# GNN layer 2: two of every 64 gathered tiles fetched by SP and ACT with one-row DMAs

## What is computed

```
h = maximum(layernorm(x), 0)
H = einsum('ni,rio->rno', h, W)
msg = (H[etype, src] + b[etype]) * weight
x = x + relu(segment_sum(msg, dst))
```

## Time and profile before

| | us |
|---|---|
| median of three runs | 8151.24 (8143.28 to 8152.59) |
| span of the profiled execution, first to last instruction | 8149.0 |
| PE busy | 6825.6 (84%) |
| POOL busy | 6074.5 (75%) |
| DVE busy | 3995.9 (49%) |
| ACT busy | 1919.9 (24%) |
| mean granted clock of TensorE | 0.932 |

### The profile page before, as it was taken

The page is one execution under the profiler, slowest core; times in us unless marked ns, Lnnn a source line. Parts: engine busy times, 40 slices in busy tenths (PEclk is TensorE's granted clock), DMA queues, the critical chain, the costliest instruction groups (busy, mean ns, idle before and its releaser), DMA issues.

```text
span 8149.0 us, 187072 instructions
## 1 busy us (share of the span) xinstructions
PE 6825.6 (84%) x52884; PEld 5276.0 (65%) x52884; DVE 3995.9 (49%) x13480; ACT 1919.9 (24%) x4919; POOL 6074.5 (75%) x6335
## 2 busy tenths in 40 slices
PE   5999999999999999999967777777778877777777
PEld 4666666666666666666646666666666666666665
DVE  7333333333333333333365555555555556555554
ACT  2333333333333333333330000000000000000001
POOL 5777777777777777777757777777777777777776
PEclk7999999999999999999979888888888888988898
DMA  6333333333333333333322222222222222222222
GB/s 141 82 83 82 81 83 82 83 82 83 82 83 82 82 83 82 83 83 82 82 61 53 53 53 53 53 53 52 53 53 53 53 52 53 52 53 53 53 53 72
DMA packets 797549, 566.94 MB, mean 70 GB/s; under 512 B 481443, under 2 KB 671019, under 8 KB 797292
## 3 DMA queue, kind: packets, MB, share of 16 engines
q0 software_dynamic: 200192, 256.65, 14.6%
q1 hardware_dynamic: 597340, 310.10, 14.5%
HBM read 544.45 MB, written 21.68 MB: 69 GB/s over the span
## 4 chain that ended last, share of the span: by engine, by line
PE 32%; issue 24%; POOL 21%; DMA 20%; DVE 1%; POOLq 1%; SPq 0%; ACT 0%; DVEq 0%; ACTq 0%
PE bank L1130 19%; POOL shared L549 17%; DMA shared<-p_tab,idx 11%; DMA rows_place<-h_tab,idx 6%; PE bank L1143 5%; POOL rows_place L549 4%; PE bank L1132 3%; DMA idx<-in_src_t 2%; PE bank L1054 2%; PE bank L1145 1%; PE bank L1061 1%; PE bank L1080 0%; DMA x_in<-in_x 0%; PE bank L1071 0%; DVE stats L744 0%
## 5 line engine op out<-in xcount | busy, mean ns | idle before, releaser
L549 POOL DMA_INDIRECT shared<-p_tab,idx x3128 | 2984.1, 954 | 959.8 <-issue 826.7
L549 POOL DMA_INDIRECT rows_place<-h_tab,idx x3128 | 2978.3, 952 | 964.3 <-issue 804.4
L1130 PE MATMUL bank<-shared,rows_place 128*128 128x256 f32 x6256 | 1842.2, 446 | 860.4 <-issue 748.1
L1130 PEld LDWEIGHTS bank<-shared,rows_place 128*128 128x128 f32 x6256 | 1296.4, 218 | 1126.6 <-issue 782.8
L959 DVE TENSOR_SCALAR shared<-iota_key,key,w_f 128x256 f32<-128x256 f32 x3128 | 1139.1, 425 | 745.3 <-PE bank L1132 633.1
L704 ACT ACTIVATE x_in<-bank 128x256 f32<-128x256 f32 x782 | 300.8, 385 | 3591.9 <-PE bank L1132 3264.7
L1061 PE MATMUL bank<-h_sb,w_tile 128*128 128x128 f32 x6256 | 907.7, 288 | 22.3 <-DVE h_sb L870 0.8
L1061 PEld LDWEIGHTS bank<-h_sb,w_tile 128*128 128x128 f32 x6256 | 758.5, 191 | 232.4 <-DVE h_sb L870 232.1
L1080 PE MATMUL bank<-wn_half,h_sb 128*128 128x128 f32 x6256 | 890.3, 285 | 0.0
L870 DVE TENSOR_SCALAR h_sb<-bank 128x128 f32<-128x128 f32 x782 | 228.2, 292 | 1315.8 <-PE bank L1054 1294.3
L1143 PE MATMUL bank<-x_in,w_rel_sb 128*128 128x64 f32 x6256 | 862.8, 296 | 0.0
(11 more groups left out here) (105 smaller groups left out, 5379.0 us busy)
## 6 DMA issues: line engine op xcount, KB each, us to landing
rows_place<-in_dst_c SPq DMA_DIRECT2D x782, 192.0 KB
shared<-in_edge_cols SPq DMA_DIRECT2D x782, 128.0 KB
shared<-p_tab,idx POOLq DMA_INDIRECT x3128
rows_place<-h_tab,idx POOLq DMA_INDIRECT x3128
idx<-in_src_t SPq DMA_DIRECT2D x1564, 2.0 KB
qr_w<-qr_tab SPq DMA_DIRECT2D x782, 18.0 KB
x_in<-in_x SPq DMA_DIRECT2D x14, 448.0 KB, 4.7
h_tab<-x_in SPq DMA_DIRECT2D x14, 448.0 KB, 3.0
```

Source lines behind the costliest of these rows:

```text
L549: pool.indirect_dma_start(out=rows_of[s][:, t, :], out_offset=None, in_=table, in_offset=bass.IndirectOffsetOnAxis(ap=idx[s][:, t:t + 1], ...
L1130: pe.matmul(bank[s][:, 0:RW], rows[s][:, t, :], hot_rel[s % 2][:, t, :], start=(t == 0), stop=(t == TC - 1))
```

## The change

In layer 2, the chunks are counted in groups of SUP = 16. In each group tiles 0 and 1 of chunk number 13 are no longer gathered by POOL. SP fetches tile 0 and ACT tile 1, row by row: for each chunk that either passes, it reads eight source numbers into registers with one call and issues eight DMAs, each of one row of h_tab to one partition. 16 such pieces fill a tile. The rows go to a place of their own with two halves, one for each of two successive groups (parts of h and hT, which layer 2 does not use). The source numbers come to partition 0 by a small strided DMA, issued by SP at chunk 5 of the group before. SP's last piece belongs to its step for chunk 13 (it waits for the slot's earlier scatter and issues the idx load first), ACT's to its step for chunk 12 (behind the copies of that chunk). Ahead of the loop SP issues two pieces and ACT three. 782 is 48 x 16 + 14, so the last chunk is such a chunk as well. The loops of SP, POOL, ACT and PE now hold 32 chunks in one turn; DVE's is unchanged.

```diff
+    SUP = 16
+    NSUP = NCH // SUP
+    ROWS = P // SUP
+    FED_AT, FED = 13, 2
...
+        fed_rows = h[0][:, 0:2 * FED, :].rearrange("p (k f) d -> p k f d", f=FED)
+        fed_ids = h[0][0:1, 2 * FED:3 * FED, :].rearrange("p f d -> p (f d)").bitcast(i32)
+        fed_ids = [fed_ids, hT[0:1, 0:FED * P].bitcast(i32)]
...
+        def feed(eng, f, lone, piece, landed):
+
+            _, at = nc.values_load_multi_w_load_instructions(
+                fed_ids[lone.half][0:1, f * P + piece * ROWS:f * P + (piece + 1) * ROWS], engines=(eng.engine,),
+                min_val=0, max_val=NPAD - 1, skip_runtime_bounds_check_because="a source node's number is below the number of nodes")
+            for k, row in enumerate(at):
+                p = piece * ROWS + k
+                eng.dma_start(fed_rows[p:p + 1, lone.half, f, :], h_tab[ds(row, 1), :]).then_inc(landed[lone.half], 16)
+
+        def feed_step(eng, f, lead, u, lone, after, landed):
+
+            first = FED_AT - lead - SUP + 1
+            if u - first < SUP:
+                feed(eng, f, lone, u - first, landed)
+            elif after:
+                if u == first + SUP:
+                    eng.wait_ge(fed_ids_landed, 16 * after.ids_turn + 16)
+                    hold(eng)
+                feed(eng, f, after, u - first - SUP, landed)
+
+        def feed_first(eng, f, lead, m, landed):
+
+            eng.wait_ge(fed_ids_landed, 16 * Lone(m, 0, 0).ids_turn + 16)
+            hold(eng)
+            for piece in range(SUP - 1 - FED_AT + lead):
+                feed(eng, f, Lone(m, 0, 0), piece, landed)
...
             def layer1_pass(m):
-                def step(c):
+                def load_ids(lone):
+                    sp.dma_start(fed_ids[lone.half], src_t[:, ds((lone.k * SUP + FED_AT) * TC, FED)].rearrange("p o -> o p"),
+                                 allow_slow_non_contiguous=True).then_inc(fed_ids_landed, 16)
+
+                def step(c, u, lone, after):
                     s = c.slot
                     sp.wait_ge(scattered[s], c.turn + 1)
                     hold(sp)
                     sp.dma_start(idx[s][:, :], src_t[:, ds(c.i * TC, TC)]).then_inc(idx1_landed[s], 16)
-
-                all_chunks(sp, m, step)
+                    if u == 5 and after:
+                        load_ids(after)
+                    feed_step(sp, 0, 0, u, lone, after, sp_row_landed)
+
+                load_ids(Lone(m, 0, 0))
+                feed_first(sp, 0, 0, m, sp_row_landed)
+                superchunks(sp, m, step)
...
+            def step1(c, u, lone, after):
+                gather(c, h_tab, rows, scattered, idx1_landed, rows_landed, range(FED if u == FED_AT else 0, TC))
+
             with pool.Fori(0, passes) as m:
-                all_chunks(pool, m, lambda c: gather(c, h_tab, rows, scattered, idx1_landed, rows_landed))
+                superchunks(pool, m, step1)
...
+                act.activation(w_sums[half][:, k, :], bank[c.slot][0:R, RW:RW + W], ACT.Copy)\
+                   .then_inc(sums_copied[c.slot], 1)
+                feed_step(act, 1, 1, u, lone, after, act_row_landed)
...
-                pe.wait_ge(rows_landed[s], 16 * TC * c.turn + 16 * TC)
+                pe.wait_ge(rows_landed[s], 16 * tiles_gathered(c, u, lone))
+                if u == FED_AT:
+                    pe.wait_ge(sp_row_landed[lone.half], 16 * P * lone.turn + 16 * P)
+                    pe.wait_ge(act_row_landed[lone.half], 16 * P * lone.turn + 16 * P)
```

More of the change, by code:

```diff
@@ L233, in gnn_two_layers @@
         pass1_ready, pass1_step = sem("pass1_ready"), sem("pass1_step")
+        fed_ids_landed, sp_row_landed, act_row_landed = sem("fed_ids_landed"), slot_sems("sp_row_landed", 2), slot_sems("act_row_landed", 2)
         block = ctx.enter_context(nc.Block())
@@ L270, in __init__ @@
                 self.m, self.slot, q = m, u % SL, quad + u // SL
+                self.quad = q
                 self.i = q * SL + self.slot
@@ L297, in paired, with __init__, superchunks @@
             step(None, at(NPAIR - 1), None)
+        assert NSUP % 2 == 0 and NCH == NSUP * SUP + FED_AT + 1
+        LONE_USES = [NSUP // 2 + 1, NSUP // 2]
+        class Lone:
+            def __init__(self, m, two, half):
+                self.m, self.half = m, half
+                self.k = two * 2 + half
+                self.turn = m * LONE_USES[half] + two
+                self.ids_turn = m * (NSUP + 1) + self.k
+        def superchunks(eng, m, step):
+            with eng.Fori(0, NSUP // 2) as two:
+                for half in range(2):
+                    for u in range(SUP):
+                        step(Chunk(m, two * (2 * SUP // SL) + (half * SUP + u) // SL, u % SL), u, Lone(m, two, half),
+                             Lone(m, two + half, 1 - half))
+            for u in range(NCH - NSUP * SUP):
+                step(Chunk(m, NSUP * SUP // SL + u // SL, u % SL), u, Lone(m, NSUP // 2, 0), None)
@@ new lines, in tiles_gathered @@
+        def tiles_gathered(c, u, lone):
+            if c.slot != FED_AT % SL:
+                return TC * c.turn + TC
+            return (c.m * (TC * SLOT_USES[c.slot] - FED * (NSUP + 1)) + lone.k * (TC * SUP // SL - FED)
+                    + (TC * (u // SL + 1) - FED * (u >= FED_AT)))
+        def feed(eng, f, lone, piece, landed):
[5 more added lines that the diff above has]
+                eng.dma_start(fed_rows[p:p + 1, lone.half, f, :], h_tab[ds(row, 1), :]).then_inc(landed[lone.half], 16)
@@ L540, in _, with gather @@
             pool.iota(pass_i[:, :], [[W, MAXPASS]], base=0, channel_multiplier=0).then_inc(ramps_set, 1)
-            def gather(c, table, rows_of, used, idx_there, landed):
+            def gather(c, table, rows_of, used, idx_there, landed, tiles=range(TC)):
                 s = c.slot
@@ L547, in gather @@
                 hold(pool)
-                for t in range(TC):
+                for t in tiles:
                     pool.indirect_dma_start(
@@ L696, in _, with copy_sums @@
             act.activation(et_key[:, :], et_key[:, :].bitcast(i32), ACT.Copy, scale=float(KEY), bias=1.0).then_inc(edges_set, 1)
[L699 to L707, removed]
-            with act.Fori(0, passes) as m:
[L710 to L714, removed]
+            def copy_sums(c, u, lone, after):
+                half, k = c.slot // 2, c.slot % 2
+                if k == 0:
+                    act.wait_ge(projected[half], c.m * HALF_USES[half] + c.quad + 1)
+                act.wait_ge(scattered[c.slot], c.turn + 2)
+                act.activation(rel_sums[half][:, :, k, :],
+                               bank[c.slot][:, 0:RW].rearrange("p (r n) -> p r n", n=W), ACT.Copy)
+                act.activation(w_sums[half][:, k, :], bank[c.slot][0:R, RW:RW + W], ACT.Copy)\
+                   .then_inc(sums_copied[c.slot], 1)
+                feed_step(act, 1, 1, u, lone, after, act_row_landed)
+            for b in range(2):
+                act.wait_ge(x_in_moved[b], 2 * MOVES)
+            with act.Fori(0, passes) as m:
+                feed_first(act, 1, 1, m, act_row_landed)
+                superchunks(act, m, copy_sums)
             for b in range(2):
@@ L1119, in _, with scatter @@
             all_groups(pe, lambda k: transpose_agg(k, k.it, mid_added))
-            def scatter(c):
+            def scatter(c, u, lone):
                 s = c.slot
                 pe.wait_ge(hot1_built[s], c.turn + 1)
-                pe.wait_ge(rows_landed[s], 16 * TC * c.turn + 16 * TC)
+                pe.wait_ge(rows_landed[s], 16 * tiles_gathered(c, u, lone))
+                if u == FED_AT:
+                    pe.wait_ge(sp_row_landed[lone.half], 16 * P * lone.turn + 16 * P)
+                    pe.wait_ge(act_row_landed[lone.half], 16 * P * lone.turn + 16 * P)
                 pe.wait_ge(sums_copied[s], c.turn + 1)
                 for t in range(TC):
-                    pe.matmul(bank[s][:, 0:RW], rows[s][:, t, :], hot_rel[s % 2][:, t, :], start=(t == 0), stop=(t == TC - 1))
+                    there = fed_rows[:, lone.half, t, :] if u == FED_AT and t < FED else rows[s][:, t, :]
+                    pe.matmul(bank[s][:, 0:RW], there, hot_rel[s % 2][:, t, :], start=(t == 0), stop=(t == TC - 1))
                 for t in range(TC):
@@ L1146, in project, with step1 @@
                   .then_inc(projected[p.half], 1)
-            def step1(pair, before, after):
+            def step1(pair, before, u, lone):
                 if pair:
-                    for c in pair.chunks:
-                        scatter(c)
+                    for k, c in enumerate(pair.chunks):
+                        scatter(c, u + k, lone)
                 if before:
                     project(before)
+            PAIRS = SUP // 2
             with pe.Fori(0, passes) as m:
-                paired(m, pe, step1)
+                at = lambda i, two=0: Pair(m, two * PAIRS + i // 2, i % 2)
+                step1(at(0), None, 0, Lone(m, 0, 0))
+                with pe.Fori(0, NSUP // 2) as two:
```

(6 more changed lines are left out.)

## The result

The changed kernel takes 8178.1 us (median of six runs, 8171.7 to 8186.5) against 8150.6 us before in the same comparison: a ratio of 1.0034, 95% interval 1.0024 to 1.0044. It is slower by about 28 us, where 107 us less were forecast. The profiled execution took 8180.6 us, with a span of 8178.8 us.

The account below looks back on a forecast made before the run. POOL was taken to bound layer 2. 8149.0 - 120.6 (gathers removed) + 10.2 (start) + 3.4 (end) = 8042, given as 8044 us for the median; range 8020 to 8550, the forecast's own 8020 to 8110.

Parts of the forecast that it names:

- the 4.87 us a chunk: POOL in layer 2: mean time per chunk once two of 64 gathers go, 4.87 instead of 5.03 us.
- the ends: Start and end of layer 2: +10.2 us before the first gather, +3.4 us at the fed last chunk.
- The hole: PE's stop at each fed chunk, until ACT's last row lands 6.0 us after the scatter of chunk 12.
- SP's step: SP's work per layer-2 chunk: index load 0.60, register load 0.47, eight rows 3.35, hold and loop 0.06; 4.5 us.
- The eight-value register load: SP's read of eight row numbers per chunk: 0.47 us with dispatch, ends 0.29 and 3.5, the least secure term.
- x: Cost of each further value in SP's register load; POOL leads up to 0.05 us, slower than before from 0.075.
- rival 1: The eight-value load is dear and SP becomes the bound of layer 2: 8546 us, or 8450; chance 0.32.
- The code: Instruction-fetch stalls in SP's long loop: 1.65 us, say four per lap of 32 chunks, 0.2 us a chunk.
- The id load: SP's load of source numbers once per group of 16 chunks: at most 0.05 us per chunk.
- the hole is real, but it costs POOL nothing: At the fed chunk: POOL would start gather 17 1.3 us after its index lands, so it loses no time.
- rival 2: PE's stop at fed chunks reaches POOL, if landing takes 4 us or ACT's piece 6: 8163 us; chance 0.11.
- T: The end of the scatter of chunk 12, from which times around a fed chunk are counted.

Follow-up runs that it names:

- run 7: Changed kernel with index loads for four chunks at once, sixteen values per SP register load and ACT's pieces one chunk earlier: 8027.0 us, ratio 0.9857.
- run 3: Changed kernel without ACT's feed, tile 1 of each fed chunk multiplied without its rows: 8126.6 us, ratio 0.9983.
- run 5: Changed kernel with each of ACT's pieces issued one chunk earlier, SP left as it is: 8136.4 us, ratio 0.9989.
- run 2: Changed kernel without SP's feed, tile 0 of each fed chunk multiplied without its rows: 8071.6 us, ratio 0.9924.

## Why the prediction was wrong

**What held.** The bound before, the price of a gather, and the 4.87 us a chunk were right: once SP's step is short enough (run 7), 117 us are gained where 120.6 less 13.6 us for the ends were summed. The start is cheaper there, because the first index load goes out ahead of SP's two pieces. The one-row issue was taken at 0.224 us and measures 0.228; a row with its address came to 0.42 and measures (3.14 - 0.23) / 7 = 0.416. ACT does hold until the scatter and then issues beside its copies. The hole's length and its place in ACT's last piece were right: 5.6 us in the median, 6.0 forecast.

**What failed first: SP's step, 4.5 us, "fits, by 0.4".** It is 5.00 without a single wait (run 3). SP's shortest steps take 4.67 us, and 0.33 a chunk come on top:
- The eight-value register load. I took 0.47 with its dispatch; it is 0.717 without it. The text called it the least secure term and kept near the low end. This is 0.25 too little; the other terms of the sum were together 0.08 too high, which gives 4.67. x of rival 1 is (0.717 - 0.432) / 7 = 0.041 us against the single load, and 0.056 between eight and sixteen values.
- The code. I named stalls of 1.65 us, four per lap, 0.2 us a chunk, and then left them out of the sum. Measured are 2.8 us once per lap of 32 (0.09 a chunk) and eight pauses of 0.35 (0.08): 0.17 a chunk, so the size that I had named was about right. No run took the code away from SP with its feed left in place, but the packets of instructions that come with each pause show that it belongs to the fetching of code.
- The id load. I allowed 0.05 a chunk; the two steps of a lap that hold one are 1.4 and 1.8 us longer than the shortest (part of that is a pause in the second and the register instruction named next), about 0.08 a chunk for the load alone. Its issue takes 0.72 to 0.74, and the eight-value load behind it takes 1.03 instead of 0.72 (run 3).
- A register instruction (L567) for the count that SP waits for, in every second step, which the sum did not have: 0.14 us each time, 0.07 a chunk.

With 5.00 instead of 4.5, SP passes POOL's 4.87 and nearly meets the 5.03 of before. That is rival 1 in what happened, but not in its cause. By its own rule, 4.5 + 7x, the measured x of 0.041 gives 4.79 and would have left POOL in the lead. I had priced this rival by the register load alone; it came by several small terms.

The account then closes: (5.00 - 4.87) x 781 is about 100 us, the hole on top of a full SP is 36, and the forecast of 8044 with both added is 8180, where 8178.1 was measured.

The rule of the Trainium skill (Runtime: NRT & Kernel Launch, Instruction fetch mechanics) for the load, about 200 ns per register in bulk, would make eight 1.6 us, as an estimate. Here, with the data in SBUF, eight take 0.717 and sixteen 1.166, so the rule is right that the price grows with the number and too high by a factor of over three for each further value (0.041 to 0.056 us). The Trainium skill's rule in the same section, that a taken branch to a block no longer held must be fetched first, agrees with the 2.97 us at the end of a lap, beside 0.25 to 0.35 elsewhere, and with the packet of instructions inside each such stop of run 3.

**What failed second: "the hole is real, but it costs POOL nothing".** It costs about 40 us (42 in run 3, 37 in run 5, 36 of gaps in run 2). Neither condition of rival 2 was met: PE went on 1.9 us after ACT's last issue in the chunk shown and 1.5 in the median, not 4, and ACT's piece ended at T + 4.0, not T + 6. The count for one fed chunk held for most of them; what failed was to let one stand for all. In run 2, where SP is free, the gaps are of two kinds. At eight of 48 fed chunks POOL was further ahead of PE than counted: it would have reached the fourth chunk behind at T + 8.4 to T + 13.0, not T + 13.9, and lost 19 us there in sum, with the gather starting at T + 12.0 to T + 13.7, where T + 12.6 was forecast for the index. At five the projection too ran at the lower clock, scatter 14 ended at T + 18.3 to T + 19.9 instead of T + 14.6, where 1.7 us were spare, and POOL lost 17 us at the fifth chunk behind. With SP full nothing was spare anywhere. That the forecast's sentence can hold is shown by run 7: a hole of 5.0 us and no cost.

**Luck.** 8178 us lies inside the stated range of 8020 to 8550, but nothing in the prediction led to it. The forecast's own range ended at 8110, rival 2 at 8163, and rival 1 was priced at 8450 or 8546.

**The ends.** Ahead of the first index load SP takes 12.4 us (4170.55 to 4182.91), 10.2 forecast. The profiled execution also reached layer 2 some 6 us later than the one before. In runs 3 and 7 the first id loads are issued at 4158 and 4164 us, so this differs from one execution to the next and is not shown to be the change's.

## What to carry over

When work is taken off the bound and given to an engine with idle time, compare its whole new step with the shorter period, in every part: the loads into registers by their number, what a long unrolled loop costs in late code, and what comes once per lap. Here a margin of 0.37 us in 4.87 was used up by four terms of 0.07 to 0.25, and a stall that one has named belongs in the sum. The helper then needs relief rather than the bound: 0.43 us a chunk taken off SP by an edit that alone is worth nothing in the kernel before was here worth 1.5%. And a count made for one place in the trace should be checked against several of them.

## What the runs showed of the hardware

- A register load of n values from SBUF on SP took 0.432 us for one, 0.717 for eight and 1.166 for sixteen. On ACT eight took 0.724.
- A one-row DMA (512 bytes, HBM to one partition) costs SP 0.228 us to issue and ACT 0.213, and with a computed address one goes out about every 0.41 us. From the last of eight issues to PE's start were 1.9 us in the fed chunk shown, 1.5 in the median.
- After PE had stood for 5.9 us its granted clock was 0.50 for scatter 13, the projection and scatter 14, 12.7 us from 6121.19 on. That is not the rule: after waits of 5.0 to 7.8 us at 48 fed chunks the projection was slow (3.68 us) in 9 and back at 2.0 to 2.6 in 39. After the 2.85 us gap of the earlier trace rows only the scatter was slow, too. What decides between them is not shown.
- A loop of 32 chunks on SP, 956 instructions long, paused every 128 instructions for 0.34 to 0.40 us and for 2.4 to 2.9 us at each return to its start (run 3), each time with a packet of 8 KB on the queue of instructions. SP's loop of four chunks had no such pauses, and 0.12 us at its return.
